# Six batches of a routed MLP carried inside the delta rule's units, and the key convolution taken off TensorE

## The reference, cut to what matters

```
# layer 2, second half: routed MLP, for every batch
h = layernorm(x) * (1 + cb) + sb
route = argmax of two gate scores
y = shared MLP(h) + MLP[route](h)          # each 128 -> 512 -> 128, relu
x = x + gb * y
# layer 3, first half: gated delta rule, for every batch
h = layernorm(x) * (1 + ca) + sa
q = silu(conv4(h @ Wq)); k = silu(conv4(h @ Wk)); v = silu(conv4(h @ Wv))   # conv4: 4 taps along time, one filter a channel
state = a * (state - b * (state k) k^T) + b * v k^T ; out = state q          # token by token, 8 heads
x = x + ga * (rms(out) * silu(h @ Wg)) @ Wo
```

## Time and profile before

| | |
|---|---|
| median of 3 runs | 4078.03 us (4077.9 to 4082.77) |
| the profiled execution, its own time | 4057.76 us |
| span of the profiled execution | 4056.0 us |
| mean granted TensorE clock | 0.865 of 2.4 GHz |
| PE busy | 3493.4 us, 86% |
| DVE busy | 2420.1 us, 60% |
| ACT busy | 1594.6 us, 39% |
| POOL busy | 537.9 us, 13% |

### The profile page before, as it was taken

The page is one execution under the profiler, slowest core; times in us unless marked ns, Lnnn a source line. Parts: engine busy times, 40 slices in busy tenths (PEclk is TensorE's granted clock), DMA queues, the critical chain, the costliest instruction groups (busy, mean ns, idle before and its releaser), DMA issues. The chain is left out here.

```text
span 4056.0 us, 124079 instructions
## 1 busy us (share of the span) xinstructions
PE 3493.4 (86%) x55256; PEld 2208.0 (54%) x55256; DVE 2420.1 (60%) x6248; ACT 1594.6 (39%) x2941; POOL 537.9 (13%) x564
## 2 busy tenths in 40 slices
PE   3877777679999999999987796999999999999985
PEld 1326665225555555555556442566666666666672
DVE  3757776337776666777675112566666666666545
ACT  1653333355443344444321243444444344444323
POOL 1212222000000000000000000222222222222210
PEclk9996667788888889889765697999999999999967
DMA  2000000121111111111000001000000000000000
GB/s 88 0 0 1 1 1 1 43 72 47 51 31 44 34 44 39 39 45 39 13 3 3 17 0 44 2 3 3 3 2 3 3 3 2 3 3 3 2 3 23
DMA packets 37029, 77.11 MB, mean 19 GB/s; under 512 B 7696, under 2 KB 11152, under 8 KB 35472
## 3 DMA queue, kind: packets, MB, share of 16 engines
q1 hardware_dynamic: 36496, 69.17, 5.3%
HBM read 64.83 MB, written 4.33 MB: 17 GB/s over the span
## 5 line engine op out<-in xcount | busy, mean ns | idle before, releaser
L1366 PE MATMUL ps<-g_hs,g_fc 128*128 128x512 f32 x448 | 282.5, 716 | 38.3 <-ACT g_hidden L1488 21.1
L1488 ACT ACTIVATE g_hidden<-ps 128x512 f32<-128x512 f32 x224 | 133.3, 595 | 391.4 <-PE ps L1366 390.8
L2133 PE MATMUL ps<-d_hp,d_w_k 128*128 128x512 f32 x512 | 281.1, 635 | 0.0
L1257 PEld LDWEIGHTS ps<-g_Q,g_K 32*32 32x32 f32 x12288 | 193.1, 113 | 142.7 <-issue 55.0
L2211 POOL TENSOR_TENSOR d_sq<-d_QK 128x512 f32<-128x512 f32 x128 | 133.1, 1040 | 930.0 <-ACT d_QK L2262 768.7
L1380 PE MATMUL ps<-g_hidden,g_proj 128*128 128x512 f32 x448 | 251.4, 656 | 0.0
L1257 PE MATMUL ps<-g_Q,g_K 32*32 32x32 f32 (+1 forms) x12288 | 223.9, 217 | 31.0 <-DVE g_H L1526 10.0
L2231 ACT ACTIVATE d_F<-ps 128x128 f32<-128x128 f32 x256 | 70.8, 276 | 345.4 <-PE ps L2042 342.2
L1225 POOL COPY g_xb<-X 128x512 f32<-128x512 f32 x8 | 7.3, 907 | 1242.6 <-DVE X L1686 1131.5
L1366 PEld LDWEIGHTS ps<-g_hs,g_fc 128*128 128x128 f32 x448 | 81.7, 214 | 150.2 <-ACT g_hidden L1488 79.5
L2406 DVE SCALAR_TENSOR_TENSOR d_conv<-ps,w_conv_q,d_conv 128x511 f32<-128x511 f32 (+2 forms) x192 | 142.3, 741 | 34.8 <-ACT d_conv L2256 30.9
(11 more groups left out here) (479 smaller groups left out, 7885.3 us busy)
## 6 DMA issues: line engine op xcount, KB each, us to landing
g_hs<-gate_rows SPq DMA_DIRECT2D x56, 256.0 KB, 3.5
g_fc<-in_c_fc_dram SPq DMA_DIRECT2D x56, 256.0 KB, 3.9
g_proj<-in_c_proj_dram SPq DMA_DIRECT2D x56, 256.0 KB, 2.8
X<-in_x_dram SPq DMA_DIRECT2D x1, 2048.0 KB, 10.8
w_c_fc<-in_c_fc_dram SPq DMA_DIRECT2D x1, 2048.0 KB, 7.9
w_c_proj<-in_c_proj_dram SPq DMA_DIRECT2D x1, 2048.0 KB, 12.3
ex_root<-gate_rows SPq DMA_DIRECT2D x1, 2048.0 KB, 14.7
h_rows<-k SPq DMA_DIRECT2D x1, 2048.0 KB, 6.3
```

Source lines behind the costliest of these rows:

```text
L1257: ins = e.matmul(later(scored, n_), keys_, queries(n_, planes, r_, 4 * i + j), start=(turn_ == 0 and part == 0 and n_ != 1), stop=(part == 1),
L1366: e.matmul(P[2], fc[:, n % 2, ts(f, C)], hs[:, n % 2], start=True, stop=True).then_inc(pe.steps, pe.did(now(f"u{i}")))
L1488: e.activation(r[:, slot], P[2], ACT.Relu).then_inc(act.steps, act.did(now(f"r{i}")))
L2133: ins = e.matmul(b, w_k[:, j, ts(H, C)], hp_of(u)[:, j:j + T], start=(j == 0), stop=(j == TAPS - 1))
```

## The change

Four things change.

1. `routed_mlp` does only batches 0 and 1.
2. Batches 2 to 7 are done in `delta_units`, batch b+2 while the units of batch b run, in 15 slots (w = 0 to 14) of two to three turns each, one per half chunk. An even slot starts at t5, an odd one at t0 (of the next chunk). Slots 0 to 2 make the norm, the mask and the score; slots 3 to 14 are 12 groups, each one MLP, one half of the columns (256) and two slices of the hidden layer. A group uses the bank of the keys (even w) or of the queries (odd w) while the projection's own use of it pauses: products up into its left half, products down into its right half.
3. Keys are projected by one product and convolved like the queries: the product at t8 place 2, ACT's multiply at t0 place 1, DVE's three adds at t0, t1 and t2 place 2, silu at t3 place 2 as before. The stage `delta_taps1` and `d_w_k` are gone.
4. `Wqk3` and the filters `conv_qk3` are loaded with the other weights of the delta rule; `delta_start` also makes the gate column and the bias.

The diff, cut to its core:

```diff
@@ in pieces_at
-                    elif x % 8 >= 4:
-                        put(u, turn, "taps", x, place={8: 0, 0: 0, 1: 1}.get(turn % NI, 2))
-                for x in range(0, 8, 2):
+                    elif x % 8 == 4:
+                        put(u, turn, "taps", x)
+                for x in range(8):
                     for j in range(TAPS):
-                        put(u, NI * (x // 2) - 50 + (0, 0, 1, 3)[j], "conv", TAPS * x + j, place=(1 if j == 0 else 2))
+                        put(u, NI * (x // 2) - (50, 45)[x % 2] + (0, 0, 1, (3, 2)[x % 2])[j], "conv", TAPS * x + j, place=(1 if j == 0 else 2))
+            for b in range(FIRST, B):
+                for w in range(2 + 1 + len(GROUPS)):
+                    turn = TU * 2 * (b - FIRST) + 12 + NI * (w // 2) + (2, 6)[w % 2]
+                    if w == 0:
+                        steps = ((0, 1, "center"), (0, 2, "square"))
+                    elif w == 1:
+                        steps = ((0, 1, "mean"), (1, 1, "root"), (2, 2, "normed"), (4, 2, "h"))
+                    elif w == 2:
+                        steps = ((0, 1, "score"), (0, 2, "mask0"))
+                    else:
+                        steps = ((0, 1, "up0"), (0, 2, "relu0"), (1, 1, "up1"), (1, 1, "down0"), (1, 2, "relu1"), (2, 1, "down1"), (2, 2, "part"))
+                    if w == 10:
+                        steps += ((2, 2, "mask1"),)
+                    for later, place, step in steps:
+                        put(0, turn + later, "mlp", (b, w, step), place=place)
@@ PE
+                        elif step in ("up0", "up1"):
+                            (p_, half, pair), j = GROUPS[w - 3], int(step[2])
+                            if j:
+                                e.wait_ge(act.steps, act.at(f"{place}relu0"))
...
+                            e.matmul(bank_[:, 0:256], k.w["w1_2"][:, p_, ts(2 * pair + j, C)], moving, start=True, stop=True,
+                                     skip_group_check=True).then_inc(pe.steps, pe.did(place + step))
+                        elif step in ("down0", "down1"):
+                            (p_, half, pair), j = GROUPS[w - 3], int(step[4])
+                            e.wait_ge(act.steps, act.at(f"{place}relu{j}"))
+                            e.matmul(bank_[:, 256:512], k.w["w2_2"][:, p_, 2 * pair + j, :], rect[:, j], start=(j == 0), stop=(j == 1),
+                                     skip_group_check=True).then_inc(pe.steps, pe.did(place + step))
@@ ACT
+                        elif step in ("relu0", "relu1"):
+                            e.wait_ge(pe.steps, pe.at(place + ("up0", "down0")[j]))
+                            e.activation(rect[:, j], bank_[:, 0:256], ACT.Relu, bias=k.w["b1_2"][:, p_, f:f + 1]).then_inc(act.steps, act.did(place + step))
@@ DVE
+                        elif step == "part":
+                            row, part = flat(k.X[:, b:b + 1, :])[:, ts(half, 256)], bank_[:, 256:512]
+                            e.wait_ge(pe.steps, pe.at(f"{place}down1"))
...
+                            e.scalar_tensor_tensor(row, part, of(GB), row, ALU.mult, ALU.add).then_inc(dve.steps, dve.did(f"m{b}part{w}"))
@@ in build
-                routed_mlp(k)
+                routed_mlp(k, 2)
```

More of the change, by code:

```diff
@@ L1702, in gla, with routed_mlp @@
         units()
-def routed_mlp(k):
+def routed_mlp(k, batches):
     nc = k.nc
@@ L1719, in routed_mlp @@
         x = lambda b: k.X[:, b, :]
-        order = [(b, p_, f) for b in range(B) for p_ in (2, 0, 1) for f in range(4)]
+        order = [(b, p_, f) for b in range(batches) for p_ in (2, 0, 1) for f in range(4)]
         NEXT = {3: "center", 6: "mean", 9: "score"}
@@ L1757, in _ @@
                         down(i - 2)
-                    if b + 1 < B and i % 12 in NEXT:
+                    if b + 1 < batches and i % 12 in NEXT:
                         prepare(b + 1, NEXT[i % 12])
@@ L1822, in _ @@
                 masks(0)
-                for b in range(1, B):
+                for b in range(1, batches):
                     norm(b)
@@ L1827, in _ @@
                     masks(b)
-                out(B - 2)
-                out(B - 1)
+                out(batches - 2)
+                out(batches - 1)
         k.end()
@@ L1863, in delta_rule @@
         q = small
+        mlp_h, mlp_t, masked = k.sb("m_h2", [C, T], stack=s), k.sb("m_t2", [C, T], stack=s), k.sb("m_masked2", [C, T], stack=s)
+        rect = k.sb("m_r2", [C, 2, T // 2], stack=s)
+        dw, gate_w, bias = k.sb("m_dw2", [C, 1], stack=s), k.sb("m_gate2", [C, C], stack=s), k.sb("m_bias2", [C, 1], stack=s)
+        FIRST, GROUPS = 2, [(p_, half, pair) for p_ in (2, 0, 1) for half in range(2) for pair in range(2)]
         pe, act, dve, pool, dma = k.stage("delta_start")
-        w_plain = QK[:].rearrange("p c h t -> p (c h t)")[:, 20 * T:].rearrange("p (c f) -> p c f", c=2)
         with nc.Block() as block:
[L1868 to L1871, removed]
             @block.scalar
@@ L1884, in delta_rule @@
         k.end()
[L1885 to L1900, removed]
         f2 = lambda ap: ap.rearrange("p h t -> p (h t)")
@@ L2236, in prepare @@
                         four = lambda n: q[n][:, :, hs]
-                        if what == "norm" and x == 1:
+                        if what == "mlp":
+                            mlp(*x)
+                        elif what == "norm" and x == 1:
                             e.wait_ge(pe.steps, pe.at(tag + "nc"))
@@ L2393, in prepare @@
                         four = lambda n: q[n][:, :, hs]
-                        if what == "norm" and x == 3:
+                        if what == "mlp":
+                            if x[2] in ("normed", "h", "mask0", "mask1", "part"):
+                                mlp(*x)
+                        elif what == "norm" and x == 3:
                             b = u // 2
@@ L2645, in build @@
                 load(k, a, "mlp2", s)
-                routed_mlp(k)
-        if first <= 5 <= upto:
-            with ExitStack() as s:
+                routed_mlp(k, 2)
                 load(k, a, "delta", s)
```

124 lines of the change are left out of this document (95 added, 29 removed).

## The result

The changed kernel took **4307.53 us** (median of 4 runs, 4297.11 to 4321.59) against 4077.97 us (4 runs, 4075.55 to 4082.77) for the kernel before beside it: a ratio of 1.0566, 95% interval 1.0537 to 1.0595. I had forecast 4059 us, with 4130 us as the upper end. The sign was wrong and the time lies 178 us above the range.

The account below looks back on a forecast made before the run. PE was taken to bound the routed MLP and the delta rule's units, there in alternation with DVE and ACT. Terms -138 - 12 + 101 + 9 + 6 + 15 = -19 us gave 4078 - 19 = 4059 us, range 3970 to 4130.

Parts of the forecast that it names:

- The stage that shrinks: Routed MLP stage: six batches leave it, each 23.0 us of a full PE, -138 us.
- the preparation: `delta_start`: weight load, filter spread and four large multiplies go, a gain of 9 to 15 us, taken as 12.
- The run-up: Before the first chunk of the units: a pair of runs takes 9 us instead of 7.6, +6 us.
- An odd group: t0 to t2: relu 0 waits behind exp and multiply on ACT, delaying PE's inverse products; 1.4 us a group.
- An even group: t5 to t7: relu 1 stands behind ACT's copies and delays the finish; 0.43 + 0.96 = 1.4 us a group.
- The granted clock: In the units: eight or nine falls to 1.2 GHz, in chunks with projections but no MLP, +15 us.
- groups 101: In the units: 72 groups of MLP work at 1.4 us each, 101 us.
- slots 9: In the units: three light slots and the empty sixteenth of a batch, 1.5 us together, x 6 = 9 us.
- upper bound of 98 us: Units: most that clock falls could cost, one fall in each of 56 chunks at 1.75 us.
- The second rival: Clock falls in most chunks, at t8 and t1; 4142 us at one a chunk, sign a clock under 0.95; chance 0.24.
- Keys' part in chunks without MLP: nothing: Chunks without MLP: adds ahead of the solve's copies cost 0.3 us, the freed t8 gives 0.25 back; nothing net.
- DVE as the bound of t0 to t2: t0 to t2: DVE's adds delay the solve beyond the wait for ACT, 2 us a group, 4102 us; chance 0.12.

Follow-up runs that it names:

- the keys alone: Changed kernel, but all eight routed MLP batches stay in their own stage; keys still get one product and are convolved on ACT and DVE: 4308.7 us.
- the kernel by one tap: Kernel before with only the last of the four products of each key projection issued, nothing added to any engine: 4278.9 us.
- the spare products: Products of 512 columns whose result nobody reads, added where key products were taken away; three per key run in the changed kernel: 4218.1 us.
- the reordered kernel: Changed kernel with the MLP's steps and the keys' first multiply moved ahead of the turns' own work on ACT, same work: 4178.3 us.

## Why the prediction was wrong

- **The stage that shrinks, the preparation:** right, -139.0 for -138, -14.6 for -12. **The run-up:** from the first product of the units to the first solve it took 85.1 us against 75.8, +9.3 for +6.
- **An odd group:** the mechanism was right, place by place: exp, multiply, relu 0, `up1`, `down0`, inverse product. A relu of 256 columns took 0.47 us, not 0.38; counted from solve 0, the inverse product came 1.35 us later in the group shown. The next one, with 2.03 us of PE idle behind relu, came 3.52 us behind solve 0, 1.7 us later than in the earlier trace rows, where I had 1.8. **An even group:** from make to finish it took 5.4 us (3025.04 to 3030.45) where I had 4.96. How much of the units' growth is the groups' can't be read from the parts: the kernel after against the keys alone gives 126 us, 1.75 us a group with a gain in clock included and 3.2 without it (1499 against 1268), but both are counted against a kernel without key taps, and my 1.4 against one that has them.
- **The granted clock: this step failed.** I took "eight or nine falls" of 1.75 us, +15 us. There were 57 between 2440 and 4080 us, of 9.6 us. Half of the 577 us of additional low time is 288 us. What is left of the +379, some 91 us, stands for my 116 (groups 101, slots 9, run-up 6). So by this estimate the sum of all terms but one was right within 25 us, and the one was off by up to 273. The near hit is for the sum only: it sets a gain of the keys' part against a higher cost of the MLP's, which I had not counted apart.
- **Why it failed.** First the count. I looked for stretches without a large product and found them only in chunks without MLP ("every stretch in MLP chunks keeps some product of 0.4 to 0.85 us"). That did not hold the clock here: the kernel by one tap keeps a key product and a query product a chunk and spends half of the units at 1.2 GHz. Second the price. I priced a fall by the one near 3158, 3.4 us long, in a chunk that still had its large products to recover with. The same trace had five more in the last chunks, without projections, of 7 to 44 us; I used these for their place and not for their length. Where the large products are gone the clock also comes back late (13.7 us in the fall at 3001.5 above). I also read the fall's surroundings too narrowly: it began at 3157.6, behind a key product at 3153.69 and inside the next one at 3157.34. My upper bound of 98 us, one fall a chunk at 1.75, inherited this and was no bound.
- **The second rival** named the cause and the places (t8 and t1) with a chance of 0.24, and its sign came (a clock of 0.81 in the units, for "under 0.95"). It would have been wrong in its time too, 4142 us, by the same price. What I held against it was the error.
- **"Keys' part in chunks without MLP: nothing"** followed from the same step. The added multiply and adds cost 15 to 50 us over all units by the two comparisons above; the missing taps alone made the units 205 us longer.
- **DVE as the bound of t0 to t2:** not what happened; PE's waits for DVE aren't the large ones in the list above.

Still open: what in PE's work, the small products or the idle times of 0.2 to 2 us between them, lets the clock fall. A product taken out leaves both behind, and one given back removes both, so the runs show that its absence costs the clock and not by which of the two. It also wasn't tried to put useful work of the right size into t8; the spare products are no way to a faster kernel, only a way to see the cause. If the reordered kernel's units had the low time of the kernel before, they would last about 1733 - (559 - 119) / 2 = 1513 us, and the kernel some 3960 us. That is an estimate that no run reached.

## What to carry to other kernels

TensorE's work in a stage that it nearly fills isn't only cost: before taking large products out, look at what is left around each place in the list, and take the price of a clock under 1.00 from every stretch of the trace that has it, the last chunks too, not from one stray fall. Taking the work out and adding nothing (one line, one run) tells the clock's share before anything is built. And when a wait is removed, look for who is late next: here the relu's place was taken by the last add into the bank.

## What the runs showed of the hardware

- 192 products of 512 columns less on TensorE made the kernel 200 us slower (ratio 1.0486, 1.0451 to 1.0522), with nothing else changed; PE was busy 1502 us instead of 1383.
- By one tap, at 3001.5, the clock fell where PE was busy 1.77 us of the 2 us from 2998 and 1.64 us of the 2 us from 3000, with no idle time above 0.36 us, in a stretch of small products. 43 of that kernel's 52 falls had an idle time of 0.5 to 1.49 us in the 4 us ahead. An idle time of 2.03 us at 3034.5 to 3036.6 in the kernel after had no fall behind it (the inverse product after it took 0.45 us), as 6 of its 13 idle times of 2.0 us or more hadn't, while 7 had one within 4 us.
- In the reordered kernel, one unread product of 512 columns per key run, in t8, cut the low time from 559 to 239 us and the kernel by 94 us.
- At the low clock, products of 128 and 512 columns took 1.8 to 2.0 times as long (2.08 for 1.16 and 1.02 us), 32 products of 32x32 only 1.4 times (0.65 for 0.45 us).
- The same kernel's time moves with its clock: thirteen executions of the kernel before, beside the last of these kernels, ran from 4060 us at a mean granted clock of 0.865 to 4105 us at 0.852, 45 us for some 106 us of low time (2 x 0.013 x 4080).
